# Four attention layers on one core: the first head's loads on two queues, the later growth of the maxima's lead, and a new order of clearing

## The chip, the cores and the metric

The kernel runs on one core of a Trainium2 chip. The metric is the device time of one execution, in microseconds, as the median over several runs of the same program.

## The reference, cut to what matters

A tensor x of 256 channels by 1024 positions goes through four layers. The first three are attention with 8 heads (layers 0, 1 and 2 below); the fourth (gated energy attention over channels) is not touched.

```python
# layer 0 (head size 16); layers 1 and 2 have head size 32, biases and a group norm ahead
q, k, v = split(w_qkv @ x)
attn = (q * scale)^T k + pos[:, None] + pos[None, :]     # pos only in layer 0
attn = softmax(attn, axis=-1)
y = attn @ v^T
x = norm(x + w_proj @ y + b_proj)                         # layers 1, 2: x + w_o @ y + b
```

## The kernel before, in words

There is no scheduler: each engine's instructions stand in the order in which the code writes them, and semaphores order the engines. Names used below:

- **Projections** (`UNITS`, `projection`, `project_out`, `split`). Layer 0 has 6: q first half, k first half, k second half, q second half, and two for V. Layers 1 and 2 have 12: the same four of q and k for heads 0 to 3 (numbers 0 to 3), four for V (4 to 7), and k, k, q, q of heads 4 to 7 (8 to 11). `EARLY` says how many TensorE does before the first scores; the rest stand in `LATE_PE`, one half (chunk) per entry, by step. ScalarE writes the high part of each (qH, kH; L495), VectorE the low part (qL, kL; L652), by a subtraction. Numbers 8 to 11 overwrite qH, kH, qL and kL, so ScalarE waits ahead of number 8 until the loads of heads 0 to 3 have landed (and ahead of 10 for the second halves of q as well).
- **Stacks** (`q_stack`, `k_stack`, `load_q` L293, `load_k` L300). A head's matrices for the scores are put together by DMA, three rows of blocks per operand: high, high and low. SyncE issues them: head 0's q after the first split, its whole k after the third, then heads 1 and 2, the shift rows of unit 0, head 3, the second q halves of heads 0 and 1, the shift rows of unit 1, the second halves of 2 and 3, and so on.
- **Units and steps.** A layer has 16 units (head by half of the queries), each 8 steps; a step is one score tile of 128 x 512. For each step TensorE does a tile for the maxima (L889, `scores_for_max`), which VectorE reduces (L662), and later the tile itself (L916, `scores`), which ScalarE turns into E by exp (L514). Both go through rings of 3 PSUM banks. After a unit's 8 maxima VectorE makes negmax (L668), TensorE transposes it (L907, at `rows_step(j)`), ScalarE and VectorE write the high and low part (L503, L675) and SyncE puts the two shift rows into q_stack (L320); the unit's scores wait for that.
- **The lead.** At step s the maxima are `lead_of(s)` tiles ahead: 16 at the start, and one more at each step in `LEAD_GROWTH`, 20 from the fourth on. So maxima run alone for 16 steps (-16 to -1; below: the ramp), and a step of LEAD_GROWTH has two maxima. From step 29 TensorE does the product with V (L927), 16 matmuls every 8 steps. In layers 1 and 2 GpSimd adds pairs of E tiles (L450, L455).
- **Start of layer 0.** GpSimd clears k_stack (L379), ScalarE and VectorE clear q_stack (L465, L618), GpSimd issues the rows of ones and of positions, VectorE interpolates the positions (L621 to L638), and the constants are made on GpSimd.

```python
for s in range(-LEAD, STEPS):
    if s in ROWS_AT:
        low_rows(l, ROWS_AT[s])          # VectorE: the low shift rows first
    for i in maxima_at(s):
        maxima(l, i)
    if s in LATE_DVE[l]:
        split(l, LATE_DVE[l][s])
```

Of the kernel before, what the change touches and what calls it, by code (L numbers as in the profile page):

```python
# [45 lines left out]
REC_STEP = 64  # L46
LEAD_GROWTH = (1, 3, 5, 7)
SUMS_STEP = 29
# [18 lines left out]
def rows_step(j):  # L67
    return TILES * j - (10 if j > 2 else 6)

# [20 lines left out]
def attention_chain(nc, x, w0, w1, w2, w3, pos_bias, cols, row3, out):  # L90
    ctx = ExitStack()
    with ctx:
# [3 lines left out]
        def sem(name):  # L96
# [81 lines left out]
            sem("w_o"), sem("pos_dma"), sem("row_in"), sem("out_dma"))  # L178
        const_set, ones_set, v_ones, stacks_clear = sem("const_set"), sem("ones_set"), sem("v_ones"), sem("stacks_clear")
        pool_chain, dve_chain = sem("pool_chain"), sem("dve_chain")  # L180
# [3 lines left out]
        proj_done, v_out, high_ready, split_ready = sem("proj_done"), sem("v_out"), sem("high_ready"), sem("split_ready")  # L184
        stack_dma = [sem(f"stack_dma{h}") for h in range(NH)]
        second_dma = [sem(f"second_dma{h}") for h in range(HEADS_B)]
        a_done, a_used = sem("a_done"), sem("a_used")
# [46 lines left out]
        def stack_count(l):  # L234
            return 16 * 6 * (l + 1)

        def second_count(l):
            return 16 * 3 * (l + 1)

# [48 lines left out]

        def load_q(eng, l, h, cs, done):

            p, d, slot = head_row(l, h), HEAD_DIM[l], slot_of(h)
            for blk, src in ((0, qH), (1, qH), (2, qL)):
# [3 lines left out]
        def load_k(eng, l, h):  # L296

            p, d, slot = head_row(l, h), HEAD_DIM[l], slot_of(h)
            for blk, src in ((0, kH), (2, kH), (1, kL)):
                eng.dma_start(k_stack[d * blk:d * (blk + 1), slot, :].bitcast(F32),  # L300
                              src[p:p + d, :].bitcast(F32)).then_inc(stack_dma[h], 16)

        @block.sync
        def _(sp):
# [18 lines left out]

            first, second, both = slice(0, HALF), slice(HALF, N), slice(0, N)
            for l in range(LAYERS):
                if l:
                    sp.wait_ge(b_done, STEPS * l)
                sp.wait_ge(split_ready, QK0[l] + 1)
                load_q(sp, l, 0, first, stack_dma[0])
                sp.wait_ge(split_ready, QK0[l] + 3)  # L330
                load_k(sp, l, 0)
                for h in (1, 2):
                    load_q(sp, l, h, first, stack_dma[h])
                    load_k(sp, l, h)
                shift_rows(l, 0)
                load_q(sp, l, 3, first, stack_dma[3])
                load_k(sp, l, 3)
                sp.wait_ge(split_ready, QK0[l] + 4)
# [16 lines left out]
                for h in range(4, NH):  # L355
                    if h >= SLOTS:
                        shift_rows(l, h + 1)
                        sp.wait_ge(b_done, STEPS * l + 32 + TILES * (h - SLOTS + 1))
                    load_q(sp, l, h, both, stack_dma[h])
                    load_k(sp, l, h)  # L360
                    if h < SLOTS:
                        shift_rows(l, h + 1)
# [12 lines left out]
        def _(pool):  # L375
            pool.dma_start(pos_in[:, :, :], pos_bias[0]).then_inc(pos_dma, 16)

            pool.memset(ones[:, :], 1.0).then_inc(ones_set, 1)  # L378
            pool.memset(k_stack[:, :, :].bitcast(F32), 0.0).then_inc(stacks_clear, 1)  # L379
            pool.wait_ge(ones_set, 1)  # L380
            pool.wait_ge(stacks_clear, 3)
            for dst, r in ((q_stack, p0), (k_stack, p0 + 2), (k_stack, SHIFT_ROW)):
                pool.dma_start(dst[r:r + 2, :, :].bitcast(F32), ones[0:2 * SLOTS * N // P, :]).then_inc(one_rows_in, 16)
            pool.memset(ident[:, :], 0.0).then_inc(pool_chain, 1)
            pool.memset(V[:, :, :], 1.0).then_inc(v_ones, 1)
            pool.memset(group_avg[:, :], 1.0 / NORM_GROUP).then_inc(pool_chain, 1)
# [5 lines left out]
            pool.wait_ge(pool_chain, 3)  # L392
            pool.affine_select(out=ident[:, :], in_=ident[:, :], compare_op=ALU.not_equal, fill=1.0, base=0,
                               pattern=[[-1, P]], channel_multiplier=1).then_inc(const_set, 1)

# [11 lines left out]
                               pattern=[[-DP, P // DP], [0, DP]], channel_multiplier=1).then_inc(const_set, 1)  # L407

            for part, src in enumerate((posH, posL)):
                pool.wait_ge(pos_ready, part + 1)  # L410
                for dst, r in ((q_stack, p0 + 2 + part), (k_stack, p0 + part)):
                    pool.dma_start(dst[r:r + 1, 0:SLOTS, :].bitcast(F32), src[0:SLOTS, :]).then_inc(pos_rows, 16)

# [48 lines left out]
        def _(act):  # L462
# [33 lines left out]

            def high_rows(l, j):
# [35 lines left out]
            for l in range(LAYERS):  # L533
# [38 lines left out]
                if l < 2:  # L572
                    if l == 0:
                        act.wait_ge(const_set, 7)
# [265 lines left out]
        def _(pe):  # L840
# [35 lines left out]
            def scores_for_max(l, i):  # L876
# [3 lines left out]
                if r == 0:  # L880
                    pe.wait_ge(stack_dma[h], stack_count(l))
                    if f and g == 0:
# [78 lines left out]
            for l in range(LAYERS):  # L961
# [21 lines left out]
                if l == 0:  # L983
                    pe.wait_ge(const_set, 7)
                    pe.wait_ge(one_rows_in, 48)
                    pe.wait_ge(pos_rows, 16 * 4)
                for s in range(-LEAD, STEPS):
# [4 lines left out]
                    if s >= 0:  # L992
                        if s == 0:
                            pe.wait_ge(split_ready, QK0[l] + 2)
                        scores(l, s)
# [173 lines left out]
```

## Time and profile before

| | |
|---|---|
| median of 3 runs | 516.5 us (515.22 to 517.43) |
| the profiled execution, its own time | 514.55 us |
| its span, first to last instruction | 512.8 us |
| TensorE busy | 479.3 us, 93% |
| VectorE busy | 360.1 us, 70% |
| ScalarE busy | 273.3 us, 53% |
| GpSimd busy | 217.8 us, 42% |
| granted TensorE clock, mean | 0.98 |

Times inside the trace are microseconds from the span's start; 1.75 us of the execution's own time lie outside the span. The three layers begin their scores at about 22, 184 and 344 us. A busy time is the time in which an engine had an instruction in work; a matmul's end is modelled, so a full TensorE is not one at its peak.

### The profile page before, as it was taken

What the parts mean: (1) busy time and instruction counts of PE and PEld (TensorE: products, weight loads), DVE (VectorE), ACT (ScalarE), POOL (GpSimd) and SP (SyncE); (2) the same over time, 40 slices, a digit from 0 to 9 for tenths busy, and PEclk for the clock granted to TensorE, in tenths of its full rate; (3) what the DMA queues carried; (4) which work ended last, traced back from release to release, by engine and by line L of the source; (5) the groups of instructions that cost most, each with busy time, mean ns of one, the idle gap of its engine ahead of it and who ended that gap; (6) DMA issues with size and microseconds to landing.
All of it is one profiled execution on the core that took longest, in us unless ns stands there. A gap on an engine that the chain in (4) does not pass through costs nothing.

```text
span 512.8 us, 7031 instructions
## 1 busy us (share of the span) xinstructions
PE 479.3 (93%) x2268; PEld 238.7 (47%) x2268; DVE 360.1 (70%) x687; ACT 273.3 (53%) x522; POOL 217.8 (42%) x203
## 2 busy tenths in 40 slices
PE   8799999999989899999999999999999989998996
PEld 6454444443237565444444322664544444432463
DVE  7599888976164568987887823738988787832573
ACT  3138776767514324876766762131777765764032
POOL 8300021001000002898879991000699888896000
PEclk9969999999998998999999999998999999999999
DMA  5330432000000054487944440034457854442002
GB/s 145 56 57 20 137 65 34 1 2 2 1 0 1 15 123 104 82 203 159 207 89 84 83 79 5 1 88 109 92 120 154 182 105 83 84 83 42 1 0 82
DMA packets 16419, 38.18 MB, mean 74 GB/s; under 512 B 4870, under 2 KB 6030, under 8 KB 16256
## 3 DMA queue, kind: packets, MB, share of 16 engines
q1 hardware_dynamic: 11088, 21.72, 17.7%
q0 software_dynamic: 5152, 16.00, 16.9%
q8 instruction: 18, 0.29, 0.2%
q14 instruction: 17, 0.14, 0.1%
q10 hardware_dynamic: 144, 0.02, 0.0%
HBM read 4.76 MB, written 1.05 MB: 11 GB/s over the span
## 4 chain that ended last, share of the span: by engine, by line
PE 68%; DVE 15%; DMA 4%; ACT 4%; issue 3%; SPq 3%; POOL 2%; ACTq 0%; POOLq 0%; DVEq 0%
PE PV L927 15%; PE S L889 15%; PE S L916 11%; DVE max L662 10%; PE S L1037 4%; DMA k_stack<-kL 4%; PE M L943 3%; PE PV L844 2%; PE S L870 2%; DVE rec_sb L692 2%; PE M L870 2%; PE PV L870 2%; PE S L907 2%; PE S L1082 2%; PE PV L863 1%
## 5 line engine op out<-in xcount | busy, mean ns | idle before, releaser
L662 DVE TENSOR_REDUCE max<-S 128x1 f32<-128x512 f32 x384 | 239.8, 669 | 20.8 <-PE S L889 20.6
L514 ACT ACTIVATE E<-S 128x512 f32<-128x512 f32 x384 | 212.6, 601 | 76.2 <-PE S L916 72.2
L450 POOL TENSOR_TENSOR SUMS<-E 128x512 f32<-128x512 f32 x126 | 167.0, 1476 | 123.9 <-ACT E L514 123.8
L889 PE MATMUL S<-k_stack,q_stack 126*128 126x512 f32 x384 | 183.2, 490 | 13.5 <-DVE max L662 8.7
L916 PE MATMUL S<-q_stack,k_stack 128*128 128x512 f32 x384 | 154.6, 411 | 2.7 <-ACT E L514 1.5
L889 PEld LDWEIGHTS S<-k_stack,q_stack 126*128 126x128 f32 x384 | 74.4, 194 | 92.9 <-DVE max L662 64.7
L927 PE MATMUL PV<-E,V 128*32 128x512 f32 x768 | 95.4, 599 | 1.7 <-ACT pv_sb L521 1.7
L916 PEld LDWEIGHTS S<-q_stack,k_stack 128*128 128x128 f32 x384 | 72.6, 191 | 33.3 <-ACT E L514 20.6
L692 DVE RECIPROCAL rec_sb<-den_sb 128x64 f32<-128x64 f32 (+1 forms) x54 | 35.7, 665 | 35.0 <-ACT den_sb L531 35.0
L503 ACT ACTIVATE mHL<-S 4x128 fp32r<-4x128 f32 x48 | 12.6, 263 | 55.2 <-PE S L907 55.2
L927 PEld LDWEIGHTS PV<-E,V 128*32 128x32 f32 x768 | 20.0, 109 | 45.2 <-issue 28.3
L425 POOL TENSOR_TENSOR att<-pv_sb,rec_sb 128x512 f32<-128x512 f32 x9 | 12.9, 1432 | 61.4 <-DVE rec_sb L692 61.4
L675 DVE TENSOR_TENSOR mHL<-S,mHL 4x128 fp32r<-4x128 f32 x48 | 13.3, 278 | 35.7 <-ACT mHL L503 35.7
L455 POOL DMA_DIRECT2D SUMS<-SUMS x30 | 26.3, 877 | 9.0 <-POOL SUMS L450 8.7
L419 POOL DMA_DIRECT2D q_stack<-SUMS x6 | 3.0, 493 | 55.7 <-PE S L916 55.7
L692 DVE RECIPROCAL rec_sb<-M 128x256 f32<-128x256 f32 x6 | 10.5, 1752 | 21.5 <-PE M L949 18.2
L1037 PE MATMUL S<-att,W 128*128 128x512 f32 x48 | 21.8, 600 | 0.0
L844 PE MATMUL PV<-ones 128*128 128x128 f32 x128 | 18.2, 304 | 2.4 <-POOL ones L378 2.4
L907 PEld LDWEIGHTS S<-ident,negmax 128*4 128x4 f32 x48 | 4.0, 83 | 33.4 <-issue 26.1
L844 PEld LDWEIGHTS PV<-ones 128*128 128x128 f32 x128 | 17.3, 217 | 2.8 <-POOL ones L378 2.4
L943 PE MATMUL M<-SUMS,ones 128*32 128x512 f32 x128 | 15.8, 598 | 1.6 <-issue 1.6
L907 PE MATMUL S<-ident,negmax 128*4 128x128 f32 x48 | 13.3, 277 | 0.9 <-DVE negmax L668 0.6
(180 smaller groups left out, 335.5 us busy)
## 6 DMA issues: line engine op xcount, KB each, us to landing
SUMS<-SUMS POOLq DMA_DIRECT2D x30, 512.0 KB, 5.1
k_stack<-kH SPq DMA_DIRECT2D x32, 128.0 KB, 3.0
q_stack<-qH SPq DMA_DIRECT2D x40, 64.0 KB, 2.0
k_stack<-kL SPq DMA_DIRECT2D x16, 128.0 KB, 3.2
q_stack<-qH SPq DMA_DIRECT2D x16, 128.0 KB, 2.3
q_stack<-mHL SPq DMA_DIRECT2D x96, 2.0 KB
q_stack<-qL SPq DMA_DIRECT2D x20, 64.0 KB, 2.0
X<-x_in_dram SPq DMA_DIRECT2D x2, 512.0 KB, 5.5
```

Of the source, the lines that this page charges most:

```text
L450: pool.tensor_tensor(SUMS[:, slot, :], E[:, E_PLAN[s][0], :], E[:, E_PLAN[s + 1][0], :], ALU.add).then_inc(sum_ready, 1)
L514: act.activation(E[:, slot, :], B[:, ring_of_scores(s) % B_RING, :], ACT.Exp, scale=1.0 if l == 0 else float(HEAD_DIM[l]) ** -0.5).then_in ...
L662: dve.tensor_reduce(max8[:, m % 2, r:r + 1], A[:, n % A_RING, :], AX.X, ALU.max, negate=True).then_inc(a_used, 1)
L692: dve.reciprocal(rec_sb[:, cs], den_sb[:, cs] if b < BLOCKS - 1 else M[:, cs]).then_inc(rec_ready, 1)
L844: pe.matmul(PV[:, 0:P], ones[:, :], ones[:, :], start=True, stop=True)
L870: mm = pe.matmul(bank, W[l][:, kc, off:off + P], src[:, kc, HALF * half:HALF * (half + 1)], start=(kc == 0), stop=(kc == KC - 1))
L889: pe.matmul(A[:, n % A_RING, :], q_stack[0:SHIFT_ROW, slot, q0:q0 + P], k_stack[0:SHIFT_ROW, slot, k0:k0 + HALF], start=True, stop=True).t ...
L907: pe.transpose(B[0:4, ring_of_rows(j) % B_RING, 0:P], negmax[:, m % 2, :], ident[:, :]).then_inc(rows_done, 1)
L916: pe.matmul(B[:, ring_of_scores(s) % B_RING, :], k_stack[:, slot, P * t:P * (t + 1)], q_stack[:, slot, HALF * f:HALF * (f + 1)], start=Tru ...
L927: mm = pe.matmul(PV[DP * u:DP * (u + 1), :], V[:, t, DP * h:DP * (h + 1)], E[:, E_PLAN[32 * b + 8 * u + t][0], :], start=(t == 0), stop=(t ...
L943: mm = pe.matmul(M[DP * u:DP * (u + 1), :], ones[:, 0:DP], SUMS[:, sum_slot(first + u, k), :], start=(k == 0), stop=(k == 1 and u < folded))
L1037: mm = pe.matmul(S[:, u, :], W[l][:, kc, wo + P * c:wo + P * (c + 1)], att[:, kc, HALF * half:HALF * (half + 1)], start=(kc == 0), stop=(k ...
```

## The change

1. **First head's loads.** `load_q` and `load_k` take which blocks they load and which columns of k. Head 0's high blocks are issued by ScalarE, right behind the ScalarE instruction that writes them; SyncE issues only its low blocks. Head 0's k goes by halves: the first counts on `stack_dma[0]`, the second on a new semaphore `half_dma`, which TensorE awaits ahead of the second maxima tile.
2. **V projections.** `EARLY` is 6 in all layers (7 before in layers 1 and 2), and number 6 goes to the steps -15 and -13, number 7 to -11 and -9.
3. **Clearing.** ScalarE clears k_stack too (128 x 5120). GpSimd makes the identity and fills V first, then issues the rows of ones and of positions, and makes the other constants behind them. TensorE's first maxima wait for `ident_set` instead of all constants, and `const_set` is awaited ahead of the first scores.
4. **The lead** grows at steps 12, 20, 28 and 36 instead of 1, 3, 5 and 7, and `rows_step` for the units 3 to 6 is 18, 25, 32 and 39 instead of 14, 22, 30 and 38.

```diff
-LEAD_GROWTH = (1, 3, 5, 7)
+LEAD_GROWTH = (12, 20, 28, 36)
 def rows_step(j):
-    return TILES * j - (10 if j > 2 else 6)
+    return TILES * j - min(max(j + 3, 6), 10)
...
-        EARLY = (6, 7, 7)
-        LATE_PE = [{}] + 2 * [{-15: (7, 0), -13: (7, 1), -3: (8, 0), -1: (8, 1), 1: (9, 0), 3: (9, 1),
+        EARLY = (6, 6, 6)
+        LATE_PE = [{}] + 2 * [{-15: (6, 0), -13: (6, 1), -11: (7, 0), -9: (7, 1), -3: (8, 0), -1: (8, 1), 1: (9, 0), 3: (9, 1),
...
+        HIGH_Q, LOW_Q = ((0, qH), (1, qH)), ((2, qL),)
+        HIGH_K, LOW_K = ((0, kH), (2, kH)), ((1, kL),)
...
-                load_q(sp, l, 0, first, stack_dma[0])
+                load_q(sp, l, 0, first, stack_dma[0], LOW_Q)
+                sp.wait_ge(split_ready, QK0[l] + 2)
+                load_k(sp, l, 0, first, stack_dma[0], LOW_K)
                 sp.wait_ge(split_ready, QK0[l] + 3)
-                load_k(sp, l, 0)
+                load_k(sp, l, 0, second, half_dma, LOW_K)
...
             pool.memset(ones[:, :], 1.0).then_inc(ones_set, 1)
-            pool.memset(k_stack[:, :, :].bitcast(F32), 0.0).then_inc(stacks_clear, 1)
+            pool.memset(ident[:, :], 0.0).then_inc(pool_chain, 1)
+            pool.wait_ge(pool_chain, 1)
+            pool.affine_select(out=ident[:, :], in_=ident[:, :], compare_op=ALU.not_equal, fill=1.0, base=0,
+                               pattern=[[-1, P]], channel_multiplier=1).then_inc(ident_set, 1)
+            pool.memset(V[:, :, :], 1.0).then_inc(v_ones, 1)
...
+            act.activation(k_stack[:, :, :],
+                           ones[:, 0:1].to_broadcast([P, SLOTS * N]).rearrange("p (h n) -> p h n", n=N),
+                           ACT.Copy, scale=0.0).then_inc(stacks_clear, 1)
...
                 if c:
+                    act.wait_ge(half_dma, half_count(l))
...
                 act.activation(high, src, ACT.Identity, bias=bias, scale=scale).then_inc(high_ready, 1)
+                if n < 3:
+                    if l == 0:
+                        act.wait_ge(stacks_clear, 3)
+                    act.wait_ge(high_ready, QK0[l] + n + 1)
+                    if kind == "q":
+                        load_q(act, l, 0, first, stack_dma[0], HIGH_Q)
+                    elif half == 0:
+                        load_k(act, l, 0, first, stack_dma[0], HIGH_K)
+                    else:
+                        load_k(act, l, 0, second, half_dma, HIGH_K)
...
                     pe.wait_ge(stack_dma[h], stack_count(l))
+                if i == 1:
+                    pe.wait_ge(half_dma, half_count(l))
```

**ScalarE, the first projections of layer 1.** Ahead of the change:

```order
L495 ACTIVATE qH<-S,col 128x512 [waits proj_done]
L495 ACTIVATE kH<-S,col 128x512 [waits proj_done]
L495 ACTIVATE kH<-PV,col 128x512 [waits proj_done]
L495 ACTIVATE qH<-M,col 128x512 [waits proj_done]
L481 ACTIVATE V<-PV 128x512 [waits proj_done]
```

And now:

```order
L509 ACTIVATE qH<-S,col 128x512 [waits proj_done]
L302 DMA q_stack<-qH 32x512 [waits high_ready]
L302 DMA q_stack<-qH 32x512
L509 ACTIVATE kH<-S,col 128x512 [waits proj_done]
L309 DMA k_stack<-kH 32x512 [waits high_ready]
L309 DMA k_stack<-kH 32x512
L509 ACTIVATE kH<-PV,col 128x512 [waits proj_done]
L309 DMA k_stack<-kH 32x512 [waits high_ready]
L309 DMA k_stack<-kH 32x512
L509 ACTIVATE qH<-M,col 128x512 [waits proj_done]
```

Six DMA issues now stand between the first four ScalarE writes of the layer.

**TensorE, the end of the projections and the first maxima of layer 1** (PV and M with W,att are V projections, S<-k_stack,q_stack are maxima tiles). Ahead of the change:

```order
L863 MATMUL M<-W,att 128x256 [waits split_ready]
L863 MATMUL M<-W,att 128x256 x3
L863 MATMUL PV<-W,att 128x256 [waits v_out]
L863 MATMUL PV<-W,att 128x256 x3
L889 MATMUL S<-k_stack,q_stack 128x512 [waits a_used,stack_dma0]
L889 MATMUL S<-k_stack,q_stack 128x512 [waits a_used]
L863 MATMUL M<-W,att 128x256 [waits v_out]
```

And now:

```order
L887 MATMUL M<-W,att 128x256 [waits split_ready]
L887 MATMUL M<-W,att 128x256 x3
L916 MATMUL S<-k_stack,q_stack 128x512 [waits a_used,stack_dma0]
L916 MATMUL S<-k_stack,q_stack 128x512 [waits a_used,half_dma]
L887 MATMUL PV<-W,att 128x256 [waits v_out]
L887 MATMUL PV<-W,att 128x256
```

The V projection number 6 (in PV) stood ahead of the first maxima and now stands behind the second.

**VectorE, layer 1, from the second negmax on** (steps 0 to about 4; mHL is the low shift rows, kL the split of number 8). Ahead of the change:

```order
L668 TENSOR_REDUCE negmax<-max 128x4 [waits rows_done,a_used]
L662 TENSOR_REDUCE max<-S 128x1 [waits negmax_ready,a_done]
L662 TENSOR_REDUCE max<-S 128x1 [waits a_done] x2
L675 TENSOR_TENSOR mHL<-S,mHL 4x128 [waits rows_high]
L662 TENSOR_REDUCE max<-S 128x1 [waits a_done]
L652 SCALAR_TENSOR_TENSOR kL<-PV,col,kH 128x512 [waits high_ready]
```

And now:

```order
L692 TENSOR_REDUCE negmax<-max 128x4 [waits rows_done,a_used]
L686 TENSOR_REDUCE max<-S 128x1 [waits negmax_ready,a_done]
L686 TENSOR_REDUCE max<-S 128x1 [waits a_done]
L699 TENSOR_TENSOR mHL<-S,mHL 4x128 [waits rows_high]
L686 TENSOR_REDUCE max<-S 128x1 [waits a_done]
L676 SCALAR_TENSOR_TENSOR kL<-PV,col,kH 128x512 [waits high_ready]
```

One maximum less stands between the second negmax and the low shift rows of unit 1.

## Rows read from the trace of the kernel before

**Rows 1.** The page: busy time of each engine.
```profile
PE 479.3 (93%) x2268; PEld 238.7 (47%) x2268; DVE 360.1 (70%) x687; ACT 273.3 (53%) x522; POOL 217.8 (42%) x203
```

**Rows 2.** The chain that ended last, layer 1: start us, us, what.
```profile
182.78 1.73 PE PV L863 x8
...
189.96 0.04 DVE negmax L668
...
195.33 2.29 DMA k_stack<-kL
...
197.72 0.07 ACT kH L495
...
198.31 0.59 ACT E L514
...
199.07 0.28 DVE mHL L675
...
231.19 0.23 PE S L916
```

**Rows 3.** VectorE in order of time, layer 1: start, us, operation [idle before <-releaser].
```profile
184.78 5.15 DVE L662 TENSOR_REDUCE max<-S 128x1 f32<-128x512 f32 x8 [4.06 <-PE S L889]
...
195.11 1.29 DVE L662 TENSOR_REDUCE max<-S 128x1 f32<-128x512 f32 x2 [1.20 <-PE S L889]
...
199.07 0.28 DVE L675 TENSOR_TENSOR mHL<-S,mHL 4x128 fp32r<-4x128 f32 x1 [0.68 <-ACT mHL L503]
...
209.34 0.67 DVE L662 TENSOR_REDUCE max<-S 128x1 f32<-128x512 f32 x1
```

**Rows 4.** Layer 1 in stretches of 2 us: PE, PEld, DVE, ACT, POOL busy, PEclk, DMA.
```profile
192.00:194.00 2.00, 1.92 (x5) 1.18 (x4) 1.91 (x4) 0.00 (x0) 0.00 (x0) 0.50 0.14 35
216.00:218.00 2.00, 1.95 (x9) 0.95 (x7) 1.97 (x6) 1.94 (x5) 2.00 (x3) 1.00 0.98 186
```

**Rows 5.** SyncE's queue in order of time, layer 1.
```profile
190.78 1.38 SPq L320 DMA_DIRECT2D q_stack<-mHL  x2
...
199.76 1.28 SPq L320 DMA_DIRECT2D q_stack<-mHL  x2
...
204.21 0.59 SPq L293 DMA_DIRECT2D q_stack<-qL  x1
...
224.64 6.89 SPq L320 DMA_DIRECT2D q_stack<-mHL  x4
```

**Rows 6.** ScalarE in order of time, layer 1.
```profile
206.55 0.68 ACT L495 ACTIVATE qH<-PV,col 128x512 fp32r<-128x512 f32 x1
```

**Rows 7.** The page, DMA issues: KB each, median us from issue to landing.
```profile
q_stack<-qL SPq DMA_DIRECT2D x20, 64.0 KB, 2.0
```

**Rows 8.** All engines in order of time, the start of layer 0.
```profile
0.80 0.38 ACTq L463 DMA_DIRECT2D col<-cols_dram  x1
...
2.20 4.40 POOL L379 MEMSET k_stack<- 128x5120 f32 x1
...
2.51 2.76 ACT L465 ACTIVATE q_stack<-ones 128x3072 fp32r<-128x3072 f32 x1
4.42 2.33 DVE L621 TENSOR_SCALAR E<-E 8x256 f32<-8x256 f32 x1 [1.35 <-DMA E<-pos_dram]
6.78 0.28 DVE L622 TENSOR_SCALAR E<-E 8x256 f32<-8x256 f32 x1
...
10.74 0.60 ACT L495 ACTIVATE qH<-S 128x512 fp32r<-128x512 f32 x1 [5.47 <-PE S L870]
...
14.11 0.60 ACT L495 ACTIVATE kH<-PV 128x512 fp32r<-128x512 f32 x1 [1.12 <-PE PV L870]
...
18.27 1.95 PE L863 MATMUL M<-W,X 128*128 128x128 f32 x16
...
22.72 4.87 DVE L662 TENSOR_REDUCE max<-S 128x1 f32<-128x512 f32 x8 [5.57 <-PE S L889]
...
37.86 1.28 SPq L320 DMA_DIRECT2D q_stack<-mHL  x2
```

More of the change, by code:

```diff
@@ L185, in attention_chain @@
         stack_dma = [sem(f"stack_dma{h}") for h in range(NH)]
+        half_dma = sem("half_dma")
         second_dma = [sem(f"second_dma{h}") for h in range(HEADS_B)]
@@ L237, in second_count, with half_count @@
         def second_count(l):
+            return 16 * 3 * (l + 1)
+        first, second, both = slice(0, HALF), slice(HALF, N), slice(0, N)
+        def half_count(l):
             return 16 * 3 * (l + 1)
@@ L287, in head_row, with load_q, load_k @@
             return 16 * h if l == 0 else DP * (h % 4)
-        def load_q(eng, l, h, cs, done):
+        HIGH_Q, LOW_Q = ((0, qH), (1, qH)), ((2, qL),)
+        HIGH_K, LOW_K = ((0, kH), (2, kH)), ((1, kL),)
+        def load_q(eng, l, h, cs, done, parts=HIGH_Q + LOW_Q):
             p, d, slot = head_row(l, h), HEAD_DIM[l], slot_of(h)
-            for blk, src in ((0, qH), (1, qH), (2, qL)):
+            for blk, src in parts:
                 eng.dma_start(q_stack[d * blk:d * (blk + 1), slot, cs].bitcast(F32),
                               src[p:p + d, cs].bitcast(F32)).then_inc(done, 16)
-        def load_k(eng, l, h):
+        def load_k(eng, l, h, cs, done, parts=HIGH_K + LOW_K):
             p, d, slot = head_row(l, h), HEAD_DIM[l], slot_of(h)
-            for blk, src in ((0, kH), (2, kH), (1, kL)):
-                eng.dma_start(k_stack[d * blk:d * (blk + 1), slot, :].bitcast(F32),
-                              src[p:p + d, :].bitcast(F32)).then_inc(stack_dma[h], 16)
+            for blk, src in parts:
+                eng.dma_start(k_stack[d * blk:d * (blk + 1), slot, cs].bitcast(F32),
+                              src[p:p + d, cs].bitcast(F32)).then_inc(done, 16)
         @block.sync
@@ L322, in shift_rows @@
                                  mHL[:, m % 2, r, :].bitcast(F32)).then_inc(shift_dma[m % 2], 16)
-            first, second, both = slice(0, HALF), slice(HALF, N), slice(0, N)
             for l in range(LAYERS):
@@ L328, in _ @@
                 sp.wait_ge(split_ready, QK0[l] + 1)
-                load_q(sp, l, 0, first, stack_dma[0])
+                load_q(sp, l, 0, first, stack_dma[0], LOW_Q)
+                sp.wait_ge(split_ready, QK0[l] + 2)
+                load_k(sp, l, 0, first, stack_dma[0], LOW_K)
                 sp.wait_ge(split_ready, QK0[l] + 3)
-                load_k(sp, l, 0)
+                load_k(sp, l, 0, second, half_dma, LOW_K)
                 for h in (1, 2):
                     load_q(sp, l, h, first, stack_dma[h])
-                    load_k(sp, l, h)
+                    load_k(sp, l, h, both, stack_dma[h])
                 shift_rows(l, 0)
                 load_q(sp, l, 3, first, stack_dma[3])
-                load_k(sp, l, 3)
+                load_k(sp, l, 3, both, stack_dma[3])
                 sp.wait_ge(split_ready, QK0[l] + 4)
@@ L359, in _ @@
                     load_q(sp, l, h, both, stack_dma[h])
-                    load_k(sp, l, h)
+                    load_k(sp, l, h, both, stack_dma[h])
                     if h < SLOTS:
@@ L383, in _ @@
                 pool.dma_start(dst[r:r + 2, :, :].bitcast(F32), ones[0:2 * SLOTS * N // P, :]).then_inc(one_rows_in, 16)
-            pool.memset(ident[:, :], 0.0).then_inc(pool_chain, 1)
-            pool.memset(V[:, :, :], 1.0).then_inc(v_ones, 1)
+            for part, src in enumerate((posH, posL)):
+                pool.wait_ge(pos_ready, part + 1)
+                for dst, r in ((q_stack, p0 + 2 + part), (k_stack, p0 + part)):
+                    pool.dma_start(dst[r:r + 1, 0:SLOTS, :].bitcast(F32), src[0:SLOTS, :]).then_inc(pos_rows, 16)
             pool.memset(group_avg[:, :], 1.0 / NORM_GROUP).then_inc(pool_chain, 1)
@@ L407, in _ @@
                                pattern=[[-DP, P // DP], [0, DP]], channel_multiplier=1).then_inc(const_set, 1)
[L409 to L412, printed above, removed]
             def load_pos(h):
@@ L573, in _ @@
                     if l == 0:
-                        act.wait_ge(const_set, 7)
+                        act.wait_ge(const_set, 6)
                     else:
@@ L983, in _ @@
                 if l == 0:
-                    pe.wait_ge(const_set, 7)
+                    pe.wait_ge(ident_set, 1)
                     pe.wait_ge(one_rows_in, 48)
```

7 lines of the change are left out of this document (3 added, 4 removed).

## Prediction, made before the changed kernel ran

> **What bounds the kernel now.** I read the page first. TensorE has work in 93% of the span [rows 1], but that figure counts modelled ends, and the chain that ended last shows other engines where this change acts. So I read the chain of layer 1, then each engine in order of time there. The reader is to see four things.
>
> First, the first maxima of layer 1 wait for nothing but TensorE's program order: the V projection number 6 takes 1.73 us from 182.78 [rows 2], the first maxima tile follows at 184.51, and VectorE starts at 184.78 [rows 3].
>
> Second, from there VectorE sets the pace. Eight maxima take 4.87 us, 0.61 each, in layer 0 [rows 8] (5.15 in layer 1, with one gap [rows 3]), and in steps 12 to 28 VectorE is busy for 1.97 of 2 us while ScalarE has 1.94 and the granted clock is 1.00, 2.4 GHz [rows 4].
>
> Third, where VectorE does wait, SyncE's queue stands behind it. From the first negmax (189.96) the chain goes to the shift rows of unit 0, through the six loads of head 3 behind them, to the landing of the last at 195.33 + 2.29 = 197.62, to ScalarE's number 8, which may not overwrite kH earlier, to the next E, to the shift rows of unit 1 and to VectorE at 199.07 [rows 2]. SyncE issues without a gap from 190.78 to 204.21 + 0.59 = 204.80, and the shift rows of unit 1 go out at 199.76 in their turn [rows 5]. The last second half of q lands 2.0 us after its issue [rows 7], at 206.2, and ScalarE's number 10 starts at 206.55 [rows 6].
>
> Fourth, VectorE's waits between 184.78 and 210 that the rows show are 1.20 and 0.68 us [rows 3]. The first falls into a stretch in which the granted clock is at 0.50 [rows 4], that is 1.2 GHz, after TensorE had little to do in the ramp.
>
> My rule for the sum: a layer moves by as much as VectorE moves at the point where the same maxima are left. After step 12 it is saturated, so each maximum that is left over costs 0.61 us.
>
> **Layer 0, before the first maxima.** The k_stack clearing moves from GpSimd (4.40 us) to ScalarE. At ScalarE's rate, 2.76 us for 3072 columns, 5120 take 4.6 us, from 5.3 to 9.9 [rows 8]; its first projection comes at 10.74 [rows 8], so this costs nothing; if it ran over, the first head would move by the excess. VectorE's first position step took 2.33 us and its like 0.28 [rows 8], the first beside GpSimd's clearing, so the positions should be done some 2 to 4 us earlier, which frees VectorE for the splits. ScalarE issues six loads of its own. None like them is in the trace. Below stands ScalarE's one load at 0.38 us [rows 8], above SyncE's loads of this very kind at 0.59 [rows 5]; I take 0.59, since the kind is the same. The third ScalarE write then goes from 14.11 [rows 8] to about 14.45, its loads are out by 16.3 and land near 18.3. The two V projections still stand ahead of the first maxima (the second from 18.27 [rows 8]) and now end at about 19.4, behind that landing. Today VectorE starts at 22.72 [rows 8]; now it starts near 20.0. **First maxima: -2.7 us.**
>
> **Layer 0, steps 0 to 12.** SyncE's line from the shift rows of unit 0 to those of unit 1 keeps its length, so these go out at 37.86 - 2.7 = 35.2 [rows 8] and land at about 37.5. But step 0 is now at about 29.6, and eight steps with single maxima, 0.6 to 0.8 us each, reach step 8 at 34.5 to 36. TensorE waits for them there, and VectorE, with one maximum per step and the ring of 3, runs dry for about 1.1 us; then for 0.8 us more at the shift rows of unit 2, and 0.6 at those of unit 1. That is 2.5 of the 2.7 gained. **Layer 0: -0.1 us.**
>
> **Layers 1 and 2.** With 0.59 us per issue ScalarE's third write of k ends 0.6 us later, and each V projection waits for a split: number 4 starts 0.4, number 5 about 0.5 later. The first maxima come after number 5, at 183.3 instead of 184.51: -1.2 us (with 0.38 per issue, -1.7). Everything in SyncE's line moves by that and no more: head 3 lands at 196.4, the shift rows of unit 1 reach VectorE at 197.9. In the new order VectorE has one maximum less ahead of that wait and is done by 195.4: 2.5 us dry against 0.68 + 1.20 [rows 3]. Second, number 10 may start at 206.2 - 1.2 = 205.0, while step 8 now comes at 202.8 (step 3 behind the E that ends at 197.7, then 5 steps of two tiles at 0.24 and three late chunks at 1.73 / 2 = 0.86 [rows 2]): ScalarE waits 1.1 us there, and the shift rows of unit 2 and maximum 27 follow (an E 0.6, mHL 0.3 and 0.3, one maximum 0.6, a split 0.7), which puts the end of maximum 27 at 208.7. Today maximum 31 ends at 209.34 + 0.67 = 210.0 [rows 3]. The new order has four more left: (208.7 - 210.0) + 4 x 0.61 = +1.1; 0.2 us of it goes back because the rows of unit 3 no longer wait. **+0.9 us each, +1.8 together.** V projection 6 costs nothing in the ramp, where TensorE was half empty, and what it does for the clock is worthless, since steps 1 to 3 wait for head 3 in any case; if they didn't, up to 1.2 us per layer would come back.
>
> The other edits cost nothing: GpSimd's constants are awaited only ahead of step 0, 10 us after they are made, and the wait on half_dma finds its loads landed (issued by ScalarE until 180.1, landed at 182.1, first needed at 183.5). TensorE does as many tiles in all as before.
>
> **The sum** is -0.1 + 1.8 = **+1.7 us** on the profiled execution's 514.55, that is 516.25. That execution lies 1.95 below the median, and against 516.5 the same sum gives 518.2. The bounds: 0.38 us per issue takes 0.5 off each of the layers 1 and 2.
>
> **The rivals.**
> *A, the late growth is free.* If a second maximum at steps 12, 20, 28 and 36 fits into time that VectorE loses anyway, only the first-maxima gains are left: -2.7 - 1.2 - 1.2 = -5.1, **511.4**. For it: VectorE is busy just 70% over all [rows 1], and does wait from step 30 on beside the product with V. Against: 1.97 of 2 us busy where three of the four fall [rows 4]. Part of it would give -3.
>
> *B, SyncE's queue becomes a stall of its own,* the slower side. The shift rows of unit 4 are now transposed at step 25, not 22. Behind them stand a weight load and head 4, then the rows of unit 5, needed at step 40. Today the rows of units 5 and 6 take 6.89 us with their waits, from 224.64 on, beside GpSimd's transfers [rows 5]; step 40 is at 231.19 [rows 2]. Some 3 us later, with both issues at 2 us and 1.7 to land, they come at 233. It decides from an arrival later than about 232. Price 1.1 us in each of layers 1 and 2: +1.7 + 2.2 = +3.9, **520.4**.
>
> *C, the issues don't run side by side.* SyncE's low block and ScalarE's second high block are asked for at the same time, at 177 and 179. If one must wait for the other, ScalarE's third write slips by another 0.59 in each of three layers: +1.7 + 1.8 = +3.5, **520.0**. Nothing in the trace shows two queues issuing together. The Trainium skill (Perfetto Trace Analysis, Per-engine timelines, DMA Instruction — HWDGE) says that the descriptor generator is shared between two issuing sequencers and locked for exclusive use. By that rule C is what happens; no row here bears it out.
>
> *D, ScalarE issues at 0.38 us:* -1.0 to the sum, **517.2**, on my side of the line.
>
> **Chances.** About 0.5%, 2.6 us, is what a measurement of this kernel can tell from no change. My forecast 0.42 and D 0.11 lie within it: 0.53. A 0.26, faster. B 0.12 and C 0.09, slower: 0.21. The range reaches from A, 511.4, to B and C, 520.5; about 1 in 10 is left out at either end. The forecast alone with D would be 516 to 519.
>
> **What would show it.** The first maxima on VectorE at 20.0 (layer 0) and 1.2 us earlier than now in layer 1 from the group norm on; SyncE without a gap behind the shift rows of unit 0; a wait of about 1 us at step 8 of layer 0 for the shift rows; waits of 2.5 and 1.9 us on VectorE for mHL at steps 2 and 10 of layers 1 and 2; steps 12 to 29 longer by about 1.8 us. I am wrong if steps 12 to 29 take as long as now, if VectorE is never dry in steps 0 to 12, or if the time between the first maxima and step 38 is not longer in every layer.

## The result and the profile after

| kernel | median, us | runs | span of the profiled execution | its own time |
|---|---|---|---|---|
| before | 516.32 (515.22 to 517.43) | 4 | 512.8 | 514.55 |
| after | 522.69 (522.29 to 523.02) | 4 | 520.5 | 522.29 |

The ratio is 1.0123, with a 95% interval of 1.0099 to 1.0147: the change makes the kernel 1.2% slower. The forecast was 518.2 with a range to 520.5, so the time lies above the range, beyond the slower rivals too. One execution of one kernel below (e2, 550.72 us at a granted clock of 0.84) is left out of its time and its ratio.

The page of the kernel after answers to [rows 1]. TensorE and VectorE are busy for 1.6 and 2.5 us less in a span that is 7.7 longer, so the time went into waits, not into work:

```profile
span 520.5 us, 7053 instructions
PE 477.7 (92%) x2268; PEld 239.5 (46%) x2268; DVE 357.6 (69%) x687; ACT 275.6 (53%) x523; POOL 211.7 (41%) x202
```

I cut each layer at two marks that both kernels have: VectorE's first maximum, and the end of maximum 63, the last of unit 7. By then both leads are at 20, so both have done the same maxima. The rest goes to the start of TensorE's last scores tile of the layer.

| | layer 0 | layer 1 | layer 2 |
|---|---|---|---|
| start of the layer to first maximum | -1.0 | -1.1 | -1.1 |
| first maximum to maximum 63 | +3.7 | +3.0 | +3.3 |
| maximum 63 to the last scores | 0.0 | +1.0 | +0.2 |
| sum | +2.6 | +2.9 | +2.4 |

With 0.2 us less between layers 0 and 1 that is the 7.7 us by which the span grew. For the middle row the stretches give VectorE's busy time. Layer 1 of the kernel after, cut at maximum 31 (us, then PE, PEld, DVE, ACT, POOL busy, PEclk, DMA share, GB/s):

```profile
186.10:213.69 27.59, 24.34 (x85) 14.60 (x83) 22.82 (x42) 13.01 (x26) 9.34 (x8) 1.00 0.45 102
213.69:238.59 24.90, 23.21 (x98) 10.77 (x97) 21.67 (x41) 16.85 (x34) 20.67 (x19) 1.00 0.60 131
```

The same for the kernel before:

```profile
184.78:210.05 25.27, 23.60 (x74) 13.40 (x72) 22.80 (x42) 10.31 (x21) 8.16 (x7) 0.93 0.44 100
210.05:234.24 24.19, 23.36 (x101) 10.94 (x100) 21.50 (x41) 19.46 (x38) 21.60 (x20) 1.00 0.67 148
```

VectorE works for 44.49 us against 44.30, but stands still (is dry) for 8.00 us against 5.16: 2.3 more up to maximum 31 and 0.5 more behind it. The granted clock is 1.00 (2.4 GHz) in both stretches of the kernel after, where [rows 4] had 0.50 in the ramp; the V projection that now fills the ramp did raise the clock, and the steps waited all the same.

VectorE in order of time, layer 1, the rows that answer to [rows 3] (start, us, operation, [idle before <-releaser]):

```profile
186.10 5.28 DVE L686 TENSOR_REDUCE max<-S 128x1 f32<-128x512 f32 x8 [2.32 <-PE S L916]
...
200.51 0.28 DVE L699 TENSOR_TENSOR mHL<-S,mHL 4x128 fp32r<-4x128 f32 x1 [2.56 <-ACT mHL L527]
...
209.13 0.28 DVE L699 TENSOR_TENSOR mHL<-S,mHL 4x128 fp32r<-4x128 f32 x1 [1.94 <-ACT mHL L527]
...
210.59 3.06 DVE L686 TENSOR_REDUCE max<-S 128x1 f32<-128x512 f32 x5
```

ScalarE there shows what it waited for, the landing of head 3's loads and of the last second half of q; the second row answers to [rows 6]:

```profile
199.17 0.69 ACT L509 ACTIVATE kH<-PV,col 128x512 fp32r<-128x512 f32 x1 [1.75 <-DMA k_stack<-kL]
...
207.78 0.69 ACT L509 ACTIVATE qH<-PV,col 128x512 fp32r<-128x512 f32 x1 [1.31 <-DMA q_stack<-qL]
```

The chain that ended last now goes through SyncE's last second-half load, where [rows 2] had only head 3, and through the shift rows of unit 3 (start, us, what):

```profile
205.66 2.02 DMA q_stack<-qL
...
208.95 0.15 ACT mHL L527
209.13 0.28 DVE mHL L699
...
216.30 0.20 DVE mHL L699
216.51 3.81 DMA q_stack<-mHL
```

At the start of layer 0, to be read against [rows 8], ScalarE's write of kH begins at 14.80 and its first pair of issues takes 1.23 us, but the next two take 1.63 and 2.47. The fourth write slips from 15.83 to 18.00, its split and the second V projection (from 19.38) stand behind it, and the first maxima come at 21.70, 1.0 earlier than before, not 2.7. Four kernels below have the same code up to there, and their first maxima come at 20.93, 21.67, 22.05 and 22.10, so this gain varies from 0.6 to 1.8 us between executions:

```profile
11.17 1.23 ACTq L302 DMA_DIRECT2D q_stack<-qH  x2
12.44 0.60 ACT L509 ACTIVATE kH<-S 128x512 fp32r<-128x512 f32 x1 [1.36 <-PE S L894]
12.57 0.55 POOL L401 DMA_DIRECT2D q_stack<-SUMS  x1
...
13.12 1.63 ACTq L309 DMA_DIRECT2D k_stack<-kH  x2
...
14.80 0.60 ACT L509 ACTIVATE kH<-PV 128x512 fp32r<-128x512 f32 x1 [1.77 <-PE PV L894]
15.49 2.47 ACTq L309 DMA_DIRECT2D k_stack<-kH  x2
...
18.00 0.60 ACT L509 ACTIVATE qH<-M 128x512 fp32r<-128x512 f32 x1 [2.60 <-issue]
```

Step 8 of layer 0 waits for the shift rows of unit 1, issued at 37.20 (37.86 in [rows 8]) behind the queue:

```profile
39.56 0.50 PE L943 MATMUL S<-q_stack,k_stack 128*128 128x512 f32 x1 [2.73 <-DMA q_stack<-mHL]
```

### The profile page after: what moved, and what is told of

It reads as the page before. It is cut to its first block, busy times and chain, and to the rows that moved or that the text cites. A ratio compares the mean times of both kernels' runs of the same rounds, so it can differ in the third digit from the quotient of the medians.

```text
span 520.5 us, 7053 instructions
## 1 busy us (share of the span) xinstructions
PE 477.7 (92%) x2268; PEld 239.5 (46%) x2268; DVE 357.6 (69%) x687; ACT 275.6 (53%) x523; POOL 211.7 (41%) x202
## 4 chain that ended last, share of the span: by engine, by line
PE 58%; DVE 17%; SPq 8%; ACT 5%; DMA 4%; issue 4%; ACTq 2%; POOL 1%; DVEq 0%; POOLq 0%
PE PV L954 15%; DVE max L686 11%; PE S L916 11%; PE S L943 10%; SPq L302 5%; PE S L1064 4%; PE M L970 3%; PE PV L868 2%; SPq L309 2%; DVE rec_sb L716 2%; DMA q_stack<-mHL 2%; PE M L887 2%; DMA k_stack<-kL 2%; ACT E L538 2%; PE S L1109 1%
## 5 line engine op out<-in xcount | busy, mean ns | idle before, releaser
L916 PE MATMUL S<-k_stack,q_stack 126*128 126x512 f32 x384 | 181.2, 481 | 12.6 <-DVE max L686 8.3
L943 PE MATMUL S<-q_stack,k_stack 128*128 128x512 f32 x384 | 156.9, 417 | 11.8 <-ACT E L538 6.8
L1064 PEld LDWEIGHTS S<-att,W 128*128 128x128 f32 x48 | 8.8, 190 | 11.2 <-issue 10.9
```

The costliest lines, as they stand in the source:

```text
L916: pe.matmul(A[:, n % A_RING, :], q_stack[0:SHIFT_ROW, slot, q0:q0 + P], k_stack[0:SHIFT_ROW, slot, k0:k0 + HALF], start=True, stop=True).t ...
L943: pe.matmul(B[:, ring_of_scores(s) % B_RING, :], k_stack[:, slot, P * t:P * (t + 1)], q_stack[:, slot, HALF * f:HALF * (f + 1)], start=Tru ...
L1064: mm = pe.matmul(S[:, u, :], W[l][:, kc, wo + P * c:wo + P * (c + 1)], att[:, kc, HALF * half:HALF * (half + 1)], start=(kc == 0), stop=(k ...
```

## Experiments

Twelve kernels ran in three sets of four. The kernel before ran beside each set (medians 514.76, 515.24 and 515.24 us), so ratios compare better across sets than medians do. The changed kernel did not run again beside them. Theory L: the late growth costs, through VectorE's dry time in steps 0 to 12. Theory Q: two queues that issue at once lengthen each other.

### First set: the parts alone

**e1_old_lead**, the change with the old lead:

```diff
-LEAD_GROWTH = (12, 20, 28, 36)
+LEAD_GROWTH = (1, 3, 5, 7)
-    return TILES * j - min(max(j + 3, 6), 10)
+    return TILES * j - (10 if j > 2 else 6)
```

> The changed kernel with the lead growing at steps 1, 3, 5 and 7 again. Theory L (the later growth costs, because VectorE runs dry in steps 0 to 12 behind SyncE's queue and then has four more maxima left, 0.61 us each): each layer gets back 1.5 to 2.2 us, so 5 to 6 us under the changed kernel, near 517, about 0 to 1 us over the kernel before or a little under it. Theory Q (the loss comes from two queues that issue at once, SyncE and ScalarE waiting for each other): 0 to 1 us under the changed kernel, near 522.

Measured: 512.97 us, ratio 0.9962 (0.9944 to 0.9980). That is the side of theory L, with nearly twice the 5 to 6 us that it expected.

**e2_lead_only**, the kernel before with the late growth and the new places of the rows, and nothing else (the same four lines the other way round).

> The kernel before with the late growth of the lead and its row steps alone. Theory L: slower than before by 1.5 to 2.5 us in each of the three layers up to step 38, in all 5 to 8 us, near 523; nothing of it ahead of step 0. Theory Q: no difference, within 1 us of 516.5.

Measured: 525.04 us, ratio 1.0205 (1.0187 to 1.0222): theory L again, and more than the 5 to 8 us that it expected.

**e3_loads_only**, the kernel before with the loads of head 0 divided between ScalarE and SyncE and k by halves (the parts of the diff in load_q, load_k, the SyncE block, project_out and the waits on half_dma).

> The kernel before with ScalarE and SyncE issuing the first head's loads and k by halves, alone. Theory L: layer 0 begins its maxima about 1 us earlier, layers 1 and 2 begin them 0.6 us later, because ScalarE's six issues delay the splits for which the V projections wait; in all 0 to +1 us. Theory Q: 3 us or more slower, with SyncE's rows of 2 us and more in all layers.

Measured: 516.04 us, ratio 1.0027 (1.0008 to 1.0046).

**e4_v_clear**, the kernel before with `EARLY = (6, 6, 6)`, the V projections 6 and 7 in LATE_PE at steps -15 to -9, and the new clearing and order of constants.

> The kernel before with the V projections number 6 and 7 behind the first scores and the clearing divided anew, without the new loads and without the late growth. Theory L: the first maxima of layers 1 and 2 come 1.4 us earlier (head 0's k by SyncE lands at 183.1), those of layer 0 1.5 to 2 us earlier, and with the early growth VectorE keeps nearly all of it: 3 to 4.5 us faster than before, near 512.5. Theory Q says the same of it. A third possibility, that the chain through head 3's landing holds whatever the first maxima do, gives 0 to 1 us.

Measured: 510.09 us, ratio 0.9909 (0.9895 to 0.9924).

The growth together with its row places is the whole loss and more: taking both out of the change turns 1.0123 into 0.9962, putting both alone into the kernel before gives 1.0205. The loads lose 0.3%, the V projections and the clearing together gain 0.9%. The three parts alone add up to +1.41%, against +1.23% for the change. The gain of e4 can be told apart by layer in its trace: its first maxima in layer 0 come 1.8 us earlier (20.89), where only the clearing and the order of the constants act, and in layers 1 and 2 the time from the first projection to the first maxima tile falls from 12.08 to 10.54 and 10.52 us, where only the V projection acts. In the ramp of layer 1 the granted clock (the third number from the end) is 1.00 in e4 too:

```profile
180.74:191.23 10.49, 9.98 (x38) 6.73 (x37) 10.30 (x18) 1.73 (x4) 0.00 (x0) 1.00 0.52 119
```

### Second set: how the growth costs

**e5_rows_only**, the change with the growth at its old steps but the rows at their new places.

```diff
-LEAD_GROWTH = (12, 20, 28, 36)
+LEAD_GROWTH = (1, 3, 5, 7)
```

> The changed kernel with the lead growing at steps 1, 3, 5 and 7 again, but with the new, later places for the rows of the maxima (those of unit 3 at step 18 instead of 14, of unit 4 at 25 instead of 22, of units 5 and 6 one or two steps later). Theory L (what costs is the four maxima that are left to VectorE behind step 12): as fast as with the old growth and the old places, 512.97 us, so 512.3 to 513.7, and first maxima to step 38 in 45.4 us in layer 1. Rival S (the later rows are what the scores wait for): a good part of the 9.7 us between 512.97 and 522.69 stays, so 516 or more, with TensorE waiting for shift rows ahead of steps 24, 32 and 40.

Measured: 516.99 us, ratio 1.0033 (1.0013 to 1.0053), 0.7% above e1. I had expected no difference, so L as I had put it is too narrow: the places of the rows have a price of their own. Of the 1.6% between e1 and the change, 0.7% are the places and 0.9% the growth itself. TensorE in layer 1 of e5 shows where, at step 40, for the rows of unit 5 (in layer 2 it waits 1.51 us there, in layer 0 not at all):

```profile
228.63 0.40 PE L916 MATMUL S<-k_stack,q_stack 126*128 126x512 f32 x1
231.65 0.79 PE L943 MATMUL S<-q_stack,k_stack 128*128 128x512 f32 x1 [2.62 <-DMA q_stack<-mHL]
```

In SyncE's queue ahead of it the issues of head 4's two kH loads take 4.26 us (1.80 in the kernel before, at 220.72, and 1.25 in e1), and the rows of units 5 and 6, [rows 5] at 224.64, go out behind them; the second of unit 5 takes 3.34 us to land:

```profile
221.26 4.26 SPq L309 DMA_DIRECT2D k_stack<-kH  x2
225.56 0.65 SPq L309 DMA_DIRECT2D k_stack<-kL  x1
226.25 4.43 SPq L329 DMA_DIRECT2D q_stack<-mHL  x4
```

That is rival B of the prediction, in a kernel in which the steps come early enough to meet it. What lengthens the two issues was not tested. In the changed kernel itself the steps are late already, and no wait stands at step 40.

**e6_two_late**, two maxima late instead of four.

```diff
-LEAD_GROWTH = (12, 20, 28, 36)
+LEAD_GROWTH = (1, 3, 28, 36)
```

> The changed kernel with the lead growing at steps 1, 3, 28 and 36: two maxima late instead of four. Theory L counts maxima: the half of the cost, first maxima to step 38 longer by 1.3 us per layer than with the old growth, 46.7 in layer 1, and 517.8 us in all (516.5 to 519). Rival S, which has steps 12 and 20 as the dear ones since VectorE and ScalarE are both full there, and 28 and 36 as free since TensorE has the products with V: 513 to 514. Its opposite (28 and 36 are the dear ones) would leave 521 to 523.

Measured: 522.02 us, ratio 1.0120 (1.0091 to 1.0148). The count of maxima does not give the cost: two late ones cost as much as four. But the layers differ. In layer 1 of e6 VectorE has two maxima more ahead of the wait at step 2, which is shorter for it (1.96), but the wait at step 10 is longer, 3.35 against 1.94:

```profile
200.89 0.28 DVE L699 TENSOR_TENSOR mHL<-S,mHL 4x128 fp32r<-4x128 f32 x1 [1.96 <-ACT mHL L527]
...
211.45 0.28 DVE L699 TENSOR_TENSOR mHL<-S,mHL 4x128 fp32r<-4x128 f32 x1 [3.35 <-ACT mHL L527]
```

Together 5.31 against 4.50. Behind the longer one stands a landing, and not the order of the maxima. The chain (start us, us, what) has the last second half of q, which lands 3.96 us after its issue, where it took 2.02 in the changed kernel and 1.97 in layer 2 of e6:

```profile
206.04 3.96 DMA q_stack<-qL
```

In layer 2, without such a landing, the two waits are 2.21 and 1.40 us, together 1.15 less than the 2.81 and 1.95 of the changed kernel, which is what two maxima of 0.61 fill. Even so layers 0 and 2 get back little of the cost. Against e5, which has the same places of the rows and the old growth, e6 takes 2.4 and 1.0 us longer from the first maximum to maximum 63, and the changed kernel 3.0 and 1.7. So the two maxima at steps 28 and 36 carry more than half of the growth's cost there; why they do was not tested.

**e7_rows_first**, layer 0 of the changed kernel with unit 1's shift rows ahead in SyncE's queue.

```diff
+                if l == 0:
+                    shift_rows(l, 1)
                 sp.wait_ge(split_ready, QK0[l] + 4)
                 for h in (0, 1):
                     load_q(sp, l, h, second, second_dma[h])
-                shift_rows(l, 1)
+                if l:
+                    shift_rows(l, 1)
```

> The changed kernel, but in layer 0 SyncE issues the shift rows of unit 1 ahead of the second halves of q of heads 0 and 1. If the wait of TensorE at step 8 of layer 0 (3.04 us, VectorE dry for 2.12) is SyncE's queue, these rows go out 2 to 4 us earlier, the wait shrinks to under 1.2 and layer 0 gets 1 to 2 us shorter, kept to the end: 520.7 to 521.7 us against 522.69. Rival: what ends the wait is not the queue but the rows' own making (the eighth maximum of unit 1), or the gain is taken back at step 12 and behind: 522.3 to 523.1.

Measured: 521.59 us, ratio 1.0118 (1.0095 to 1.0141). The rows go out at 33.68 instead of 37.20 and TensorE's step 8 starts 15.3 us behind the first maximum instead of 17.9. Then the same wait stands at step 16, for the rows of unit 2, which are now behind those loads:

```profile
44.94 0.50 PE L946 MATMUL S<-q_stack,k_stack 128*128 128x512 f32 x1 [2.19 <-DMA q_stack<-mHL]
```

Maximum 39 ends 28.7 us behind the first one in this kernel and 28.9 in the changed one: 2.6 us gained, 2.4 given back. The median lies in the range that was expected for a gain, but the ratio (1.0118 against 1.0123) shows none, and in the trace 0.2 us of layer 0 are left, as the second rival had it. The queue was the cause of the wait, and taking the wait away did not take away its time.

**e8_one_queue**, the change with the old lead, where SyncE issues all loads of head 0, k by halves.

```diff
-                load_q(sp, l, 0, first, stack_dma[0], LOW_Q)
+                load_q(sp, l, 0, first, stack_dma[0])
-                if n < 3:
-                    if l == 0:
...
```

> The changed kernel with the old growth and the old places of the rows (512.97 us), but all loads of head 0 are issued by SyncE, k still by halves; ScalarE issues none. Theory Q (issues of two queues at once lengthen each other and hold back ScalarE's writes): all issues at about 0.6 us, ScalarE's writes 1.7 us apart, TensorE's first maxima tile at 20.0 to 20.6 in layer 0 instead of 21.53 and 10.5 us behind the layer's first projection instead of 10.96 in layers 1 and 2; with that 510.0 to 511.3 us, close to the 510.09 of the kernel without the new loads. Rival (the halves themselves cost, three more issues of 0.6 us ahead of the shift rows in SyncE's line): 512.5 to 514.

Measured: 512.05 us, ratio 0.9933 (0.9911 to 0.9955): between e1 and e4, nearer to e1. The places came as expected (first maxima tile at 20.35 in layer 0, 10.35 us behind the first projection in layers 1 and 2), the time did not: of the 1.2 us that layer 0 gains on e1 at the first maximum, 0.4 are lost again by maximum 63. From e4 this kernel differs by the halves of k alone, and it is 0.2% slower (the intervals overlap). So ScalarE's issues have a price ahead of the first maxima (0.6 us in layers 1 and 2; in layer 0 the kernels with them start at 20.93 to 22.10, those without them at 20.68 to 20.89), and k by halves brings nothing in return.

One expectation failed in a way that tells more. In layer 0 SyncE's issues did not all take 0.6 us, although ScalarE issues nothing here, and in the kernel before the same stands behind GpSimd's four position rows (14.95 to 17.08). First e8, then the kernel before:

```profile
14.18 2.30 SPq L309 DMA_DIRECT2D k_stack<-kH  x2
16.52 1.09 SPq L309 DMA_DIRECT2D k_stack<-kL  x1
```
```profile
17.09 1.65 SPq L300 DMA_DIRECT2D k_stack<-kH  x2
18.78 1.09 SPq L300 DMA_DIRECT2D k_stack<-kL  x1
```

So one queue with loads of GpSimd beside it is enough for long issues.

### Third set: who lengthens the issues, and can the dry time be closed

**e10_gpsimd_waits** and **e11_synce_waits**, both e1 with one line. The first holds GpSimd's seven row loads back, the second SyncE's loads.

```diff
             pool.wait_ge(stacks_clear, 3)
+            pool.wait_ge(high_ready, 4)
```
```diff
-                sp.wait_ge(split_ready, QK0[l] + 1)
+                sp.wait_ge(split_ready, QK0[l] + 4)
```

> The changed kernel with the old growth (512.97 us), but GpSimd issues its seven loads of single rows (ones and positions) only after ScalarE's fourth write of layer 0. Theory Q (SyncE's and ScalarE's issues at once lengthen each other): ScalarE's pairs of issues in layer 0 stay at 1.6 to 2.5 us. Theory G (GpSimd's row loads slow them): all three pairs take 1.15 to 1.25 us, ScalarE's fourth write starts near 16.1 instead of 18.34, and SyncE's issues behind it, at 17 to 21, are the long ones. The first maxima are not earlier than 21.5 in either, since they need those rows.

> The changed kernel with the old growth, but SyncE issues nothing of a layer until the fourth split, so that ScalarE issues alone. Theory Q: ScalarE's three pairs take 1.15 to 1.25 us each in layer 0 and the fourth write starts near 16.1. Theory G: the second and third pair stay at 1.6 to 2.5 us, the fourth write near 18. In layers 1 and 2 both expect 1.16, as now. The first maxima come 2 us or more later in every layer, so 517 to 521 us in all.

Measured, one execution each: 518.52 and 516.94 us. With GpSimd held back, ScalarE's pairs in layer 0 take 1.23, 1.15 and 1.16 us although SyncE issues beside them:

```profile
10.77 1.23 ACTq L302 DMA_DIRECT2D q_stack<-qH  x2
11.57 0.63 SPq L302 DMA_DIRECT2D q_stack<-qL  x1
12.73 1.15 ACTq L309 DMA_DIRECT2D k_stack<-kH  x2
14.61 1.16 ACTq L309 DMA_DIRECT2D k_stack<-kH  x2
15.81 0.60 ACT L510 ACTIVATE qH<-M 128x512 fp32r<-128x512 f32 x1 [1.28 <-PE M L895]
```

With SyncE held back, GpSimd's issues go from 10.39 to 14.69. ScalarE's second pair is still a long one; the third, behind them, isn't, although theory G had it long too:

```profile
11.83 1.24 ACTq L302 DMA_DIRECT2D q_stack<-qH  x2
13.65 0.53 POOL L401 DMA_DIRECT2D q_stack<-SUMS  x1
13.80 1.81 ACTq L309 DMA_DIRECT2D k_stack<-kH  x2
16.34 1.17 ACTq L309 DMA_DIRECT2D k_stack<-kH  x2
```

The first maxima of e10 come at 27.94, since they need those rows, and SyncE's pair that now stands beside them, at 19.79, takes 2.12 us. So it is GpSimd's row loads, not the second queue. How long a pair gets differs between executions. In the five kernels that have the same code there (the changed one, e1, e5, e6, e7) the first pair takes 1.22 to 1.24 us, though GpSimd issues beside it already, the second 1.16 to 2.21 and the third 1.54 to 2.47, with SyncE issuing too. That SyncE has a part in the third is seen only from e11, where it is held back and the third takes 1.17. The landings tell the same, first e1 (10 to 20 us), then e10 (10 to 17 us), KB each and median us from issue to landing:

```profile
k_stack<-kH ACTq DMA_DIRECT2D x4, 32.0 KB, 3.3
k_stack<-kL SPq DMA_DIRECT2D x2, 32.0 KB, 5.4
```
```profile
k_stack<-kH ACTq DMA_DIRECT2D x4, 32.0 KB, 1.9
k_stack<-kL SPq DMA_DIRECT2D x2, 32.0 KB, 2.2
```

**e9_late_k**, e4 with ScalarE's number 8 and its split two steps later.

```diff
-        LATE_ACT = [{}] + 2 * [{0: 8, 4: 9, 8: 10, 12: 11}]
-        LATE_DVE = [{}] + 2 * [{2: 8, 6: 9, 10: 10, 14: 11}]
+        LATE_ACT = [{}] + 2 * [{2: 8, 4: 9, 8: 10, 12: 11}]
+        LATE_DVE = [{}] + 2 * [{4: 8, 6: 9, 10: 10, 14: 11}]
```

> The kernel with the V projections behind the first scores and the new clearing alone (510.09 us), in which ScalarE's number 8 (the write of kH that waits for head 3's loads) and its split stand two steps later, behind the E of steps 1 and 2. If VectorE's wait of 1.97 us at step 2 of layer 1 is only that place in ScalarE's order, most of it goes: 1.2 to 1.9 us in each of layers 1 and 2, so 506.3 to 508.0 us. Rival: head 3's loads hold the later steps all the same (number 9, projection 10 at step 5), so that the wait appears at step 5 to 8: 509.5 to 510.5.

Measured: 509.03 us, ratio 0.9872 (0.9852 to 0.9892), the fastest of all. But the gain over e4 is 1.1 us by the medians and 0.4% by the ratios, below what was expected and above the rival's. VectorE's wait at step 2 is gone and a wait of the same size stands at step 10, behind ScalarE's number 10 and the last second half of q:

```profile
193.89 0.28 DVE L678 TENSOR_TENSOR mHL<-S,mHL 4x128 fp32r<-4x128 f32 x1 [0.24 <-ACT mHL L506]
204.39 0.28 DVE L678 TENSOR_TENSOR mHL<-S,mHL 4x128 fp32r<-4x128 f32 x1 [1.98 <-ACT mHL L506]
```

**e12_early_growth**, e4 with `LEAD_GROWTH = (0, 1, 2, 3)`.

> The kernel with the V projections behind the first scores and the new clearing alone (510.09 us), but its lead grows at steps 0, 1, 2 and 3 instead of 1, 3, 5 and 7. Theory L (what counts is VectorE's dry time of steps 0 to 12, 1.97 us at step 2 in layers 1 and 2): two more maxima stand ahead of that wait, 1.2 us less dry in each of layers 1 and 2 and almost nothing in layer 0, so 507.7 us (506.7 to 509.0). Rival: the maxima ahead of step 0 to 3 push the scores of steps 1 to 3 and with them ScalarE's E back, so that the wait only moves: 509.7 to 511.

Measured: 511.27 us, ratio 0.9915 (0.9893 to 0.9937): no gain over e4. The wait at step 2 shrinks from 1.97 to 1.37 and the one at step 10 grows from 0.34 to 1.61. The rival was right.

## Why the prediction was wrong

The span grew by 7.7 us where the sum had 1.7. Of the 6.0 us between them about 1.7 stand ahead of the first maxima of layer 0, 1.1 behind them, 0.9 and 1.2 behind step 12 of layers 1 and 2, and 1.0 and 0.2 behind maximum 63.

**What bounds the kernel** was read rightly in the main: VectorE, and behind its waits SyncE's queue. e9, e12 and e7 each shortened or removed one of these waits and found another in its place. Two readings of the trace before were not right. "After step 12 it is saturated" holds in steps 12 to 28 (VectorE is busy for 10.96 of 11.22 us there), but behind step 28 it is dry for 1.19 and 1.17 us. And "nothing in the trace shows two queues issuing together" overlooks SyncE's issues beside and behind GpSimd's position rows (the rows under e8): 1.65 us a pair and 1.09 an issue stood there to be read.

**First maxima of layer 0, -2.7: mis-sized, measured -1.0** (-0.6 to -1.8 in the four other kernels with this code). The clearing on ScalarE took 4.45 us, where 4.6 was predicted, and the positions were ready earlier. The failed step is "I take 0.59, since the kind is the same". That is the duration of an issue in a quiet stretch. The same change that moved the positions forward put GpSimd's row loads on top of ScalarE's, and two pairs took 4.10 us instead of 2.36. e4, with the earlier positions and none of ScalarE's loads, has its first maximum at 20.89. So the same clearing gains 1.8 without them, and not 2.7 either: TensorE waits there for head 0's kL, one of SyncE's loads.

**Layer 0 behind the first maxima, +2.6 (2.5 dry and the rest): measured +3.7.** The wait at step 8 was placed rightly and is larger (VectorE dry for 2.12 where 1.1 was predicted). SyncE's line from the rows of unit 0 to those of unit 1, which was to keep its length, took 9.77 us against 9.31.

**First maxima of layers 1 and 2, -1.2 each: right, -1.1.** ScalarE's writes are 1.92 us apart, with pairs of issues of 1.16.

**Steps 0 to 12 of layers 1 and 2: right, to a tenth in layer 1.** The waits of 2.5 and 1.9 us on mHL are 2.56 and 1.94 in layer 1 and 2.81 and 1.95 in layer 2. Maximum 27 ended 25.2 us behind the first one in layer 1, where the prediction's 208.7 less 183.6 is 25.1.

**Behind step 12, 4 x 0.61 - 0.2 per layer: too small.** This term was mis-sized as well, and with more weight than the first one, since it stands in two layers. By maximum 63 layers 1 and 2 are 3.0 and 3.3 us longer, where -0.1 + 2.44 - 0.2 = 2.1 was predicted. The rows of unit 3, whose waiting I had counted as a gain of 0.2, became a loss: issued four steps later, they meet GpSimd's first transfer of 512 KB (issued at 215.67) and land after 3.81 us, and TensorE waits 0.34 us for them at step 24. And e6 shows that "each maximum that is left over costs 0.61" is no rule in itself, since in layers 0 and 2 two late maxima cost more than half of what four cost. What the rest of the 0.9 and 1.2 us is stays open.

**Behind maximum 63, nothing predicted: +1.0 and +0.2** in layers 1 and 2. From maximum 63 to the last scores, layer 1 takes 76.0 us before, 76.9 after, 75.5 in e1 and 77.1 in e4, so kernels with the same order of steps there differ by as much. What sets it wasn't tried and stays open.

The sum, predicted -0.1 + 0.9 + 0.9, measured +2.6 + 2.9 + 2.4.

**The rivals.** A, the late growth free: false, e1 and e2. B, a stall of SyncE's own at unit 5: absent in the changed kernel, present in e5. C, the two queues' issues exclude each other: the lengthening is real in layer 0, the mechanism is another. In layer 1 both issue at once, for 0.33 us, and neither takes longer than alone (changed kernel, layer 1):

```profile
177.26 1.16 ACTq L302 DMA_DIRECT2D q_stack<-qH  x2
178.09 0.56 SPq L302 DMA_DIRECT2D q_stack<-qL  x1
```

The Trainium skill (Perfetto Trace Analysis, DMA Instruction — HWDGE) says that the generator is locked for exclusive use. These rows show no wait of one queue for the other; for how much of an issue the lock is held no row shows, so they do not speak against the rule, only against the 0.59 us that C took for it. D, 0.38 us per issue: false, 0.58.

The forecast's sign was right. What was missing in the range is that the terms that failed lay on the same side: those for the issues, for SyncE's line and for the rows of unit 3 each assumed that other transfers stay out of the way.

## What to carry to other kernels

Look at where the dry time of the bounding engine comes from before you reorder what fills it: in e7, e9 and e12 a wait behind SyncE's queue mostly came back at a later step when it was filled or bypassed. No kernel here made the queue shorter, so that this would help is not shown. Price a DMA issue and a landing by rows from the stretch in which they will stand, with the transfers that the same change moves there. And judge a change of several parts by its parts: here two of them gained 0.9% (1.3% with e9's two numbers) under the growth with its row places, which lost 1.6%.

## What the runs showed of the hardware

Seven loads of one or two rows issued by GpSimd (20 to 40 KB each, 416 of the 768 packets between 10 and 20 us in e1) lengthen the issues of other engines. A pair of ScalarE's issues takes 1.15 to 1.23 us in e10, where they are held back, 1.81 beside them alone (e11), and up to 2.47 where SyncE issues as well; a pair of SyncE's beside them, with ScalarE silent, takes 2.30 (e8). In e1 the 32 KB loads of k land after 3.3 and 5.4 us (medians), in e10 ahead of them after 1.9 and 2.2. In all ten kernels in which these loads go out from 10.4 on, the first pair of another engine beside them is not lengthened (1.22 to 1.26 us); the long ones begin 2.5 us and more behind GpSimd's first issue. Whether it is the number of packets or that they are GpSimd's, no run tells apart. Two hardware queues alone do not lengthen each other: ScalarE's pairs take 1.16 us in layers 1 and 2 in the changed kernel, in e10 and in e11, whether SyncE issues beside them or not.
